# Projecting q and k of the next tile one step sooner in a four-engine decoder pipeline, and moving one GpSimd group by one product

## What is computed

```python
q = sigmoid(heads(Wq, bq)); k = sigmoid(heads(Wk, bk)); v = heads(Wv, bv)
sink_in = normal / sum((q + EPS) * (cumsum(k) + EPS))
src_out = normal / sum((k + EPS) * (cumsum(q) + EPS))
...
kv = cumsum(outer(k, v * src_comp))
x  = (q * sink_in / normal) @ kv * sink_alloc
h  = layernorm(inputs + x @ Wo + bo)
a  = layernorm(h + gelu(h @ W1 + b1) @ W2 + b2)
x2 = layernorm(inputs + a)                     # the outer norm
out = layernorm(x2 + experts(x2))
```

## Time and profile before

| what | value |
|---|---|
| median of three runs | 401.84 us (401.17 to 402.3) |
| the profiled execution, its own time | 401.26 us |
| its span, first to last instruction | 399.5 us |
| TensorE busy | 366.7 us, 92% |
| VectorE busy | 331.9 us, 83% |
| GpSimd busy | 254.5 us, 64% |
| ScalarE busy | 211.3 us, 53% |
| granted TensorE clock, mean | 0.996 |

### The profile page before, as it was taken

The page is one execution under the profiler, slowest core; times in us unless marked ns, Lnnn a source line. Parts: engine busy times, 40 slices in busy tenths (PEclk is TensorE's granted clock), DMA queues, the critical chain, the costliest instruction groups (busy, mean ns, idle before and its releaser), DMA issues. The chain is left out here.

```text
span 399.5 us, 6696 instructions
## 1 busy us (share of the span) xinstructions
PE 366.7 (92%) x2056; PEld 258.8 (65%) x2056; DVE 331.9 (83%) x799; ACT 211.3 (53%) x393; POOL 254.5 (64%) x431
## 2 busy tenths in 40 slices
PE   8987999988998999899999999899999997999992
PEld 3565666865657784786668675778478664955651
DVE  2789989988689879998899979997999989834643
ACT  3340048055752886258842885278734873286450
POOL 2023849895489548983798449963898469946131
PEclk9999999999999999999999999999999999999998
DMA  8309043207300018100640038000810054000000
GB/s 259 155 12 220 6 93 93 81 1 169 96 0 2 0 42 215 38 0 2 163 126 2 2 86 205 2 1 19 203 45 1 2 137 101 2 0 29 0 26 27
DMA packets 19875, 26.59 MB, mean 67 GB/s; under 512 B 1664, under 2 KB 9984, under 8 KB 19840
## 3 DMA queue, kind: packets, MB, share of 16 engines
q1 hardware_dynamic: 19696, 25.96, 25.3%
q10 hardware_dynamic: 144, 0.21, 0.2%
HBM read 7.29 MB, written 2.10 MB: 23 GB/s over the span
## 5 line engine op out<-in xcount | busy, mean ns | idle before, releaser
L1009 POOL TENSOR_TENSOR prod<-cum_kv,q_fac 128x512 f32<-128x512 f32 x64 | 92.4, 1461 | 20.2 <-DVE cum_kv L1241 14.7
L448 PEld LDWEIGHTS pO<-s_wor,prod 128*128 128x128 f32 x512 | 63.0, 191 | 23.2 <-issue 13.0
L448 PE MATMUL pO<-s_wor,prod 128*128 128x128 f32 x512 | 67.3, 278 | 7.1 <-POOL prod L1009 6.9
L1235 DVE TENSOR_TENSOR kv<-k,vb 128x512 f32<-128x512 f32 x64 | 54.3, 849 | 1.3 <-DMA vb<-vs 1.0
L996 POOL TENSOR_TENSOR var_eps<-mv,s_con 128x4 f32<-128x4 f32 x32 | 6.8, 213 | 60.2 <-DVE mv L1263 60.2
L1241 DVE TENSOR_TENSOR_SCAN cum_kv<-p_ones,cum_kv,kv 128x512 f32<-128x512 f32 x32 | 40.6, 1277 | 0.6
L1241 DVE TENSOR_TENSOR_SCAN cum_kv<-p_ones,kv 128x512 f32<-128x512 f32 x32 | 38.8, 1216 | 0.7
L467 PE MATMUL pG<-hT,s_ffn 128*128 128x512 f32 x64 | 31.0, 607 | 2.9 <-ACT hT L835 2.2
L570 PE MATMUL pY<-s_moe,gel 128*128 128x128 f32 x256 | 33.0, 276 | 0.0
L570 PEld LDWEIGHTS pY<-s_moe,gel 128*128 128x128 f32 x256 | 31.0, 192 | 2.9 <-issue 1.9
L999 POOL TENSOR_TENSOR rstd<-var_eps,s_con 128x4 f32<-128x4 f32 x32 | 32.5, 1017 | 0.0
(11 more groups left out here) (190 smaller groups left out, 819.7 us busy)
## 6 DMA issues: line engine op xcount, KB each, us to landing
vb<-vs SPq DMA_DIRECT2D x64, 256.0 KB, 4.6
xT<-x_t SPq DMA_DIRECT2D x8, 256.0 KB, 4.1
xt<-x SPq DMA_DIRECT2D x8, 256.0 KB, 5.2
out<-y SPq DMA_DIRECT2D x7, 256.0 KB, 2.3
s_moe<-moe_w SPq DMA_DIRECT2D x1, 836.0 KB, 9.8
s_wor<-wo_rep SPq DMA_DIRECT2D x1, 512.0 KB, 7.9
s_ffn<-ffn_w SPq DMA_DIRECT2D x1, 512.0 KB, 8.3
s_con<-consts SPq DMA_DIRECT2D x1, 502.0 KB, 4.7
```

The costliest lines, as they stand in the source:

```text
L448: mm = pe.matmul(pO3[:, s, :], prod[:, m % 4, s * P:(s + 1) * P], s_wor[:, m, :], start=False, stop=(m == DH - 1), skip_group_check=True)
L1009: pool.tensor_tensor(prod[:, m % 4, :], cum_kv[t.par][:, m, :], q_fac[t.par][:, :], ALU.mult).then_inc(prod_ready, 1)
L1235: dve.tensor_tensor(kv[:, m % 3, :], k[t.par][:, :], vb[:, m, :], ALU.mult).then_inc(kv_ready, 1)
```

## The change

Two things move, and nothing is added or removed.

First, q and k of tile n = s+2 are projected in step s and not in step s+1. On TensorE the two products leave the head of the step and stand before `x2_T(c)`; `reduce_out(b, 2)`, which stood before `x2_T(c)`, now stands behind it. On ScalarE the sigmoids go behind `x2T_out(c)`. On VectorE the running sums of q and k leave their place behind `cumulate_kv(b, 7)` and go to the end of the step before, one ahead of `values(a)`, one ahead of `moments(b, 1)`. There too `outer_product(a, 2)` goes ahead of the two `second_relu`. Tile 3 is the exception: its q and k stay where they were on every engine. Waits are added so that the shared PSUM banks are not overwritten.

Second, on GpSimd `inverse_std(c, 2)` goes from behind `product(b, 2)` to between `product(b, 1)` and `product(b, 2)`, from step 3 on.

```diff
@@ TensorE, step
-                if A: project_q(a); project_k(a)
-                if D: inter_base(d, 2); inter1(d, 2); inter_base(d, 3); inter1(d, 3)
+                n = a.plus(1)
+                if D: inter_base(d, 2); inter1(d, 2); inter_base(d, 3); inter1(d, 3); inter2(d, 2)
                 if B: reduce_out(b, 1)
-                if D: inter2(d, 2); inter2(d, 3)
-                if B: reduce_out(b, 2)
+                if D: inter2(d, 3)
+                if n.exists(): project_q(n); project_k(n)
                 if C: x2_T(c)
-                if B: reduce_out(b, 3); reduce_out(b, 4)
+                if B: reduce_out(b, 2); reduce_out(b, 3); reduce_out(b, 4)
@@ ScalarE, step
-                if A: q_out(a); k_out(a)
+                n = a.plus(1)
                 if D: relu(d, 2); relu(d, 3)
                 if C: normalise(c, 2); x2T_out(c)
+                if n.exists(): q_out(n); k_out(n)
@@ GpSimd, step
-                if B and b.n > 2: product(b, 1); product(b, 2)
+                if B and b.n > 2: product(b, 1)
                 if C: inverse_std(c, 2)
+                if B and b.n > 2: product(b, 2)
@@ VectorE, step
-                if A: cumulate_q(a); cumulate_k(a)
+                if A and a.n == 3: cumulate_q(a); cumulate_k(a)
...
+                n = a.plus(1)
                 if D: piece_moments(d, 3)
+                if n.exists(): cumulate_q(n)
                 if A: values(a)
                 if D: join_moments(d, 3)
+                if n.exists(): cumulate_k(n)
                 if B: moments(b, 1)
                 if A: query_factor(a); outer_product(a, 0); cumulate_kv(a, 0)
-                if A: outer_product(a, 1); cumulate_kv(a, 1)
+                if A: outer_product(a, 1); cumulate_kv(a, 1); outer_product(a, 2)
                 if C: second_relu(c, 0); second_relu(c, 1)
-                if A: outer_product(a, 2); outer_product(a, 3); cumulate_kv(a, 2)
+                if A: cumulate_kv(a, 2); outer_product(a, 3)
@@ TensorE, the waits of project_q (project_k and project_v alike)
-                if t.n > 1:
+                if t.n in (2, 3):
                     pe.wait_ge(qfac_ready, t.n)
+                elif t.n > 3:
+                    pe.wait_ge(qfac_ready, t.n - 1)
+                    pe.wait_ge(q_ready, t.n)
```

More of the change, by code:

```diff
@@ L363, in project_k @@
                 pe.wait_ge(xT_loaded[t.par], 16 * (t.slot_uses + 1))
-                if t.n > 1:
+                if t.n in (2, 3):
                     pe.wait_ge(vs_ready, t.n)
+                elif t.n > 3:
+                    pe.wait_ge(vs_ready, t.n - 1)
+                    pe.wait_ge(k_ready, t.n)
                 if t.n == 3:
@@ L372, in project_v @@
                     pe.wait_ge(v_ready, t.n)
-                elif t.n > 1:
+                elif t.n == 2:
                     pe.wait_ge(q_ready, t.n + 1)
+                elif 2 < t.n < TILES - 1:
+                    pe.wait_ge(q_ready, t.n + 2)
+                elif t.n == TILES - 1:
+                    pe.wait_ge(qfac_ready, t.n)
                 pe.matmul(v_bank(t)[:, :], att("wv"), xT[t.par][:, :], start=True, stop=True).then_inc(v_proj, 1)
@@ L381, in head_sums @@
                 if of_q:
+                    if pair == 0 and 2 < t.n < TILES - 1:
+                        pe.wait_ge(k_ready, t.n + 2)
+                    elif pair == 0 and t.n == TILES - 1:
+                        pe.wait_ge(vs_ready, t.n)
                     pe.wait_ge((k_ready, ksrc_ready)[pair], t.n + 1)
@@ L689, in third_step @@
                 reduce_out(a, 0)
+                project_q(a.plus(1)); project_k(a.plus(1))
             def closing(c):
@@ L934, in third_step @@
                 normalise(b, 1)
+                q_out(a.plus(1)); k_out(a.plus(1))
             def closing(c):
```

## The result

| | median of the runs | ratio to before, 95% interval |
|---|---|---|
| before | 401.9 us (401.17 to 402.3) | |
| changed | 409.33 us (408.95 to 409.64) | 1.0191 [1.0179, 1.0203] |

The change makes the kernel 7.4 us slower. The direction was forecast, the size was not: 405.9 was said, with a range up to 408.8. The profiled execution of the changed kernel took 408.95 us, its span is 407.2 against 399.5.

What follows compares the result with a forecast made beforehand. It took the chain TensorE, VectorE and GpSimd, `reduce_out(b, 7)`, TensorE as the bound. 0.89 + 2 x (0.9 - 0.21) + 2 x (0.85 - 0.21) + 0.5 = 4.05 more gave 405.9 us, range 400.8 to 408.8.

Steps and rivals of the forecast that it cites:

- The direction and the chain: Slower, chance 0.67; chain: TensorE's `cumulate_e` and spreading, VectorE and GpSimd some 25 us, `reduce_out(b, 7)`, TensorE.
- Step 2, +0.89: TensorE, step 2: two added projections fit in the x2 wait, but one `reduce_out` now stands behind it: +0.89 us.
- The new wait of `inter_base`, 1.0 and covered: TensorE, start of step: outer product 2, waiting for `vb`, delays relus; new 1.0 us wait, free while product 7 is later.
- X, +0.15: VectorE, end of step: the moved running sums of q and k delay the chain by about 0.15 us a step.
- `kq`, -0.21: TensorE, steps 3 to 6: `kq` is ready early, so its wait goes, 0.21 us less per step.
- Product 7, +0.9 and +0.85: GpSimd, steps 3 to 6: product 7 ends 0.9 us later in a step like 4, 0.85 in odd tiles.
- The replay: Step 4's GpSimd and VectorE work moved through in the new order; product 7 ends at 214.2, not 213.31.
- products win ties: Rival: on tiles 3 and 5 product 3 beats outer product 6, +2.2 and not 0.85; 408.6 us, chance 0.16.
- The lock-step, +0.6 an outer product: VectorE's outer products and GpSimd's products alternate, each outer product holding GpSimd 0.6 us, none free in the root.
- The signs: Trace signs of being right: no `x2_T` wait from step 3, longer `reduce_out(b, 7)` wait, products 3 to 5 at 1.7 each.
- Last step, +0.5: Last step: the moved root and outer product put product 7 0.6 us later, 0.5 of it reaching the final `reduce_out`.
- The prediction's doubt whether products in a row can hold an outer product out: VectorE and GpSimd: by the port lock alone, back-to-back products could hold an outer product out for two; 408.6 us, chance 0.16.

Runs made afterwards that it cites:

- e6_step2: As e5_qk_only, but in step 2 alone TensorE does `reduce_out(b, 2)` ahead of `x2_T` again: 402.13 us.
- e1_root_back: The changed kernel with GpSimd's root (`inverse_std(c, 2)`) behind product 2 again: 404.41 us.
- e4_nudge: The changed kernel with one unused GpSimd addition more, ahead of product 1: 404.05 us.
- e8_nudge_root_back: The changed kernel with an added GpSimd instruction ahead of product 1, the root behind product 2, and `reduce_out(b, 2)` ahead of `x2_T` in step 2: 403.31 us.
- e2_root_alone: The kernel before with only GpSimd's root moved between products 1 and 2: 404.0 us.
- e5_qk_only: The changed kernel with the moves of outer product 2 and of the root undone, only q and k staying a step sooner: 402.76 us.
- e11_sum_first: As e5_qk_only, but TensorE does `reduce_out(b, 2)` ahead of `x2_T` in all steps: 400.6 us.
- e10: As e5_qk_only, but TensorE does `reduce_out(b, 2)` ahead of `x2_T` in steps 2 and 6: 401.36 us.
- the two with the filling: e5_qk_only and e11_sum_first, each with three unread TensorE products on constants in each of two waits (steps 3 and 6): 402.04 us and 400.63 us.
- e7_nudge_behind: The changed kernel with the same added GpSimd addition as e4_nudge, but behind product 1: 409.2 us.

## Why the prediction was right and wrong

- **The direction and the chain: right.** But for step 2's 0.99, all of the loss is in the stretch over VectorE and GpSimd up to product 7; the x2 waits that went gave back nothing, and those for `kq` some 0.4 a step.
- **Step 2, +0.89: right.** Measured +0.99, and 0.80 of it back in e6_step2.
- **The new wait of `inter_base`, 1.0 and covered: right.** It is 0.82, and as long in e1_root_back and e4_nudge, which are 5 us faster. Outer product 2 waits 0.55 for `vb`, where 0.6 was said.
- **X, +0.15: about right**, measured +0.05 to 0.15: the first outer product of tiles 4 and 5 is 1.95 and 3.42 us later than before, the `cumulate_e` ahead of it 1.9 and 3.27.
- **`kq`, -0.21: too small.** The stretch from `reduce_out(b, 7)` to `cumulate_e` got 0.46 shorter. The row of a wait counts from the modelled end of the instruction before. Undisturbed, the next starts 0.16 ahead of that end, so the wait's price is 0.21 + 0.16 = 0.37. TensorE's rows of step 4, of before and then of after (L375 and L385 `project_v`, L390 and L404 `head_sums`), show it as 1.24 and 0.86 from start to start; the group behind the wait is 0.07 shorter too (0.97 and 0.90 to the next), which with the 0.38 makes the 0.46 but for 0.01:

```profile
215.25 1.02 PE L375 MATMUL pA<-xT,s_att 128*128 128x512 f32 x2
216.49 1.13 PE L390 MATMUL pB<-s_att,kq 128*128 128x128 f32 x8 [0.21 <-DVE kq L1147]
```

```profile
218.99 1.02 PE L385 MATMUL pA<-xT,s_att 128*128 128x512 f32 x2
219.85 1.05 PE L404 MATMUL pB<-s_att,kq 128*128 128x128 f32 x8
```

- **Product 7, +0.9 and +0.85: wrong, and this is the step that failed.** Its first stretch grew by 1.63 to 1.85. The replay said "outer product 3 comes at 200.97, as `outer_residual` ends, 0.6; product 1 is 201.7". That is a tie, and it was given to the outer product without a row for it. The earlier trace rows gave who goes next once one is waiting, but not who is first when both arrive together, and e8_nudge_root_back shows that even the one that waits doesn't always go next. In the replay and in the trace of tile 4 the tie comes 7.38 us behind the tile's first outer product. Measured, product 1 began then, at the end of `outer_residual`, outer product 3 came at 7.41, and the product won in all five tiles. The prediction had even priced such a tie as a rival ("products win ties", 408.6, chance 0.16), but on two odd tiles, at product 3 against outer product 6, with 2.2 us each. The tie that was lost is another one, in all five tiles, at 1.63 to 1.85 with what follows from it. That the total lies near 408.6 is luck.
- **What the lost tie leads to was not in the replay at all.** It moved the root as 1.65 us of work and not as an instruction that waits. In the kernel before the power at 204.52 stood behind products 1 and 2, and its moments had long ended. Between products 1 and 2 nothing hides late moments. Against e4_nudge, where the root waits 0.15 us or less, product 1 ends 0.7 us earlier and the moments 1.1 later, and the sum is the 1.82 us of GpSimd's standing. So the root comes only 0.25 to 0.3 us sooner than in the kernel before (10.48 behind the first outer product of tile 4, and 10.73 before), where the prediction had 0.9 to 1.3.
- **The lock-step, +0.6 an outer product: too much.** e2_root_alone has it, with products at 1.7, and costs 0.35 and 0.47, where the replay had 0.8. So the term that came of it was too large and the tie was missing from it; the two errors partly cancelled.
- **The signs.** Products 3 to 5 were to take 1.7 each; they take 1.72, 1.26 and 1.72. `reduce_out(b, 7)` was to wait longer; it waits 0.32 as before, and the 0.55 stand at `reduce_out(b, 6)`. No wait of `x2_T` was to be left from step 3 on; step 6, in which no projection is left to fill it, has 2.17, up from 0.63.
- **Last step, +0.5: wrong with the replay**, +1.63 in the first stretch of tile 7, and the stretch from there to the end is as long as before (55.09 and 55.08).
- **The sum.** Forecast 4.05; measured 8.56 + 0.99 - 1.57 = 7.98, less the 0.28 ahead of tile 2's first outer product, which is no more than the spread of that point over all traces (94.0 to 94.9).

## What to carry to other kernels

Where a replay puts two instructions that exclude each other within a tenth of a microsecond, work it out both ways and take the worse way into the forecast: here 0.03 to 0.10 us decided over 5 us, and a useless instruction ahead of the one that had won, which let the other go first, bought them back. An instruction moved ahead of others is to be moved with its input's time, not only with its duration. And where a change empties a wait of TensorE of the work that filled it, look at the granted clock behind that wait, before the saved time is counted.

## What was not expected of the hardware

- TensorE's granted clock fell within the pipeline after single waits: 3.11 us of idle time in step 6 of e5_qk_only (0.56 behind it), 1.92 in step 3 of e11_sum_first (0.50). The 24 instructions behind it took 4.47 us in place of 2.84. It doesn't follow from the length of the wait alone: ahead of x2_T in step 6, e1_root_back idled 2.16 us and kept 1.00, and the changed kernel idled 2.17 and lost it. What else decides stays open. The four kernels with such waits and nothing to fill them (e5, e6, e10, e11) have runs that differ by 2.9 to 4.3 us, the two with the filling by 1.1 and 1.3; the kernel before, in the runs taken beside them, by 1.9 to 2.7. So the spread alone is weak evidence; the granted clocks of the single runs, above, are better. And a fall need not cost anything: the changed kernel's, which makes the 24 instructions 4.00 us long, leaves its step 6 at 23.22, as in e4_nudge, which had none (23.20).
- Between VectorE's outer product 3 and GpSimd's product 1 nothing was shared or split, however close they came: in the changed kernel and in e7_nudge_behind the outer product asked 0.03 to 0.10 us later in nine of ten tiles, and in all nine it was recorded with 1.72 to 1.79 us; in the tenth it asked 0.45 later and was recorded with 1.36.
- A VectorE instruction that stands at such a tie doesn't always go next: outer product 4 in tiles 4 and 6 of e8_nudge_root_back asked 0.13 us ahead of product 2 and ran behind it (1.94), while outer product 6 of tile 4 in the changed kernel asked 1.1 us ahead of product 5 and ran before it (1.73, the product 1.72). The prediction's doubt whether products in a row can hold an outer product out is answered by this: they can.
